# State space layer: four real products kept apart and added by TensorE, late squares and the last group's powers on GpSimd

## What is computed

```python
C_term = C * B[None]
V = jnp.exp(log_dA[:, :, None] * jnp.arange(L))
K = 2.0 * jnp.einsum('chn,hnl->chl', C_term, V).real
```

## Time and profile before

| What | Value |
|---|---|
| Time, median of 3 runs | 1275.31 us (1273.34 to 1276.65) |
| The profiled execution's own time | 1279.39 us |
| Its span | 1277.7 us |
| TensorE, share of the span | 84% |
| VectorE | 56% |
| ScalarE | 37% |
| GpSimd | 19% |
| Granted TensorE clock, mean | 0.906 of full speed |

### The profile page before, as it was taken

One profiled execution on the slowest core, in us unless ns is written; L12 is line 12 of the kernel. 1 busy time (PEld: TensorE's weight loads), 2 busy tenths in 40 slices (PEclk: granted clock), 3 DMA queues, 4 the chain that ended last, 5 costly groups with the idle time before them and its releaser, 6 DMA issues. The chain is left out here.

```text
span 1277.7 us, 22878 instructions
## 1 busy us (share of the span) xinstructions
PE 1074.6 (84%) x8418; PEld 770.7 (60%) x8418; DVE 710.4 (56%) x1761; ACT 472.6 (37%) x938; POOL 248.5 (19%) x337
## 2 busy tenths in 40 slices
PE   1227997987899888989988988988989999999990
PEld 1124665544666456766455744773548999999980
DVE  7992444675555666747577655355443444444445
ACT  2111332444365443355533655433003333333332
POOL 3970000010000001201012100002132333333320
PEclk9857998988999899799987998888889999999995
DMA  5123241019521469022806220114921111111105
GB/s 172 18 52 110 84 168 49 18 33 166 68 75 66 195 215 107 31 79 67 165 1 88 88 67 1 33 34 161 375 91 34 43 35 38 39 34 43 35 30 201
DMA packets 73419, 108.88 MB, mean 85 GB/s; under 512 B 16592, under 2 KB 58336, under 8 KB 72864
## 3 DMA queue, kind: packets, MB, share of 16 engines
q1 hardware_dynamic: 66192, 74.75, 23.4%
q0 software_dynamic: 5280, 14.57, 3.5%
q10 hardware_dynamic: 1840, 18.10, 3.5%
HBM read 83.47 MB, written 40.97 MB: 97 GB/s over the span
## 5 line engine op out<-in xcount | busy, mean ns | idle before, releaser
L1721 DVE TENSOR_REDUCE mx<-scores_ps 128x4 f32<-128x1024 f32 (+1 forms) x160 | 186.9, 1168 | 84.3 <-PE scores_ps L1193 44.0
L1549 ACT ACTIVATE pt<-turned_ps 128x1024 f32<-128x1024 f32 (+1 forms) x160 | 157.6, 985 | 146.8 <-PE turned_ps L1189 97.2
L2266 PEld LDWEIGHTS x_ps<-x_xtT,x_w1s 128*128 128x128 f32 x1248 | 145.3, 192 | 3.4 <-ACT x_xtT L2294 1.5
L2266 PE MATMUL x_ps<-x_xtT,x_w1s 128*128 128x128 f32 x1248 | 145.8, 275 | 1.0 <-ACT x_xtT L2294 1.0
L2280 PE MATMUL x_ps<-x_experts,x_hT 128*128 x624 | 141.0, 379 | 0.0
L2280 PEld LDWEIGHTS x_ps<-x_experts,x_hT 128*128 128x128 f32 x624 | 115.6, 190 | 14.2
L2309 ACT ACTIVATE x_hT<-x_ps,x_b1c 128x128 f32<-128x128 f32 x312 | 84.8, 382 | 16.6 <-issue 13.5
L1179 PE MATMUL turned_ps<-q,k 32*128 32x256 f32 x512 | 69.8, 348 | 22.4 <-DVE mx L1721 12.4
L1179 PEld LDWEIGHTS turned_ps<-q,k 32*128 32x128 f32 x512 | 42.3, 198 | 76.1 <-issue 40.6
L1064 POOL COPY vpad<-v 128x32 f32<-128x32 f32 x128 | 22.8, 223 | 311.2 <-PE ps L1230 296.4
L2329 DVE COPY x_w1s<-x_experts 128x2048 f32 x39 | 55.6, 1429 | 49.1 <-PE x_ps L2266 37.5
(11 more groups left out here) (423 smaller groups left out, 1951.4 us busy)
## 6 DMA issues: line engine op xcount, KB each, us to landing
x_slots<-x_slots ACTq DMA_DIRECT2D x4, 4160.0 KB
wexp<-in_L_ffn_w SPq DMA_DIRECT2D x16, 1024.0 KB, 5.4
x_experts<-in_L_ffn_W SPq DMA_DIRECT2D x16, 1024.0 KB, 13.7
q<-heads SPq DMA_DIRECT2D x48, 128.0 KB, 5.0
k<-heads SPq DMA_DIRECT2D x48, 128.0 KB, 10.0
ha<-h SPq DMA_DIRECT2D x16, 256.0 KB, 3.2
x_pair<-y_rows SPq DMA_DIRECT2D x4, 1024.0 KB, 9.3
heads<-nat_k_hi SPq DMA_DIRECT2D x12, 256.0 KB, 3.9
```

The lines of the kernel that those rows point to most:

```text
L1549: sc.activation(pt[v.index // 2 % (PT_RING // 2)][:, :, 0:wide], turned_ps[:, :, 0:wide], ACT.Exp)\
L1721: v.tensor_reduce(mx[:, u.group % 2, 0:blocks, u.n:u.n + 2].rearrange("p b n -> p n b"), scores_ps[:, :, 0:blocks * (P if u.causal else T) ...
L2266: last = mm(ps[2 * (i % 2) + f // KH][:, f % KH * P:(f % KH + 1) * P], w1s[:, i % 2, c, f * P:(f + 1) * P], xtT[:, i % 2, c, :], start=c = ...
```

## The change

- GpSimd no longer makes the complex product. For each token it writes four real products into `cs` (now four parts): x_r b_r, x_i (-b_i), x_r (-b_i), x_i (-b_r). The subtraction and the addition are gone, as are `csn` and the negation of each group. ScalarE negates `bs` once into `nbs`, in one operation of 128 x 1024.
- TensorE makes four matmuls per token and half in place of two (parts 0 and 1 with the real powers, 2 and 3 with the imaginary ones), all into the same PSUM columns.
- VectorE makes the first four squares only (`EARLY = 4`). GpSimd makes `dk[5]`, `dk[6]` and `dk[7]`, in five operations each.
- VectorE makes the powers of four groups. GpSimd makes those of the last one (`last_powers`), into a buffer of its own, `pw_last`, between the strided products of group 3 and of group 4. `pw_last` lies where the input tile `xin` was. ScalarE still copies the first eight powers of the last group in, at the same place of its order as before, without a wait of its own.

```diff
-    cs = [sb(f"s4_cs{i}", [P, 2, GT, CH, NA]) for i in range(2)]
-    csn = [sb(f"s4_csn{i}", [P, GT, CH, NA]) for i in range(2)]
+    cs = [sb(f"s4_cs{i}", [P, 4, GT, CH, NA]) for i in range(2)]
+    nbs = sb("s4_nbs", [P, 2, HP, NA])
...
+    EARLY = 4
+    sq = sb("s4_sq2", [P, HP])
+
+    def powers_in(g):
+        return pw_last if g == NG - 1 else pw[g % 2]
...
-            pool.wait_ge(squares, 8)
+            pool.wait_ge(squares, EARLY + 1)
+            for k in range(EARLY, 7):
+                cur, nxt = dk[k], dk[k + 1]
+                s.mark(g_.tensor_tensor(nxt[:, 0, :], cur[:, 0, :], cur[:, 0, :], ALU.mult))
+                s.mark(g_.tensor_tensor(sq[:, :], cur[:, 1, :], cur[:, 1, :], ALU.mult))
+                s.step(g_.tensor_tensor(nxt[:, 1, :], cur[:, 0, :], cur[:, 1, :], ALU.mult))
+                s.mark(g_.tensor_tensor(nxt[:, 0, :], nxt[:, 0, :], sq[:, :], ALU.subtract))
+                s.step(g_.tensor_tensor(nxt[:, 1, :], nxt[:, 1, :], nxt[:, 1, :], ALU.add))
+                pool.sem_inc(more_squares, 1)
...
+            pool.sem_inc(bases, 1)
             pool.wait_ge(columns, 4)
-            for g in range(NG):
+            pool.wait_ge(negated, 1)
+
+            def strided(g):
                 tok, count = tokens_of(g), GROUPS[g][1]
                 shape = [P, count, CH, NA]
                 if g >= 2:
                     pool.wait_ge(banks_full, g - 1)
-                    pool.wait_ge(negated, g - 1)
-                cmul(g_, s, [[t[:, i, 0:count] for i in range(2)] for t in (pt1, pt2)],
...
+                for part, (a, b) in enumerate(((xr, br), (xi, nbi), (xr, nbi), (xi, nbr))):
+                    s.mark(g_.tensor_tensor(cs[g % 2][:, part, 0:count], a, b, ALU.mult))
+                s.sync()
                 pool.sem_inc(strides, 1)
+
+            def last_powers():
+                tok, count = tokens_of(NG - 1), GROUPS[-1][1]
+                for k in range(3, 6):
+                    n = 1 << k
+                    base = [p8[:, i, tok, :] if k == 3 else pw_last[:, i, :, 0:n] for i in range(2)]
+                    if k == 3:
+                        pool.wait_ge(eighths, 1)
+                    if k == 4:
+                        pool.wait_ge(heads_in, NG)
+                    d = [dk[k][:, i, tok].unsqueeze(2).to_broadcast([P, count, n]) for i in range(2)]
...
+                    cmul(g_, s, temps, [pw_last[:, i, :, n:2 * n] for i in range(2)], base, d)
+                pool.sem_inc(powers_last, 1)
+
+            for g in range(NG - 1):
+                strided(g)
+            last_powers()
+            strided(NG - 1)
...
-            for k in range(7):
+            for k in range(EARLY):
...
-            for g in range(NG):
+            for g in range(NG - 1):
                 pg, tok, count = pw[g % 2][:, :, 0:GROUPS[g][1]], tokens_of(g), GROUPS[g][1]
...
             def first_powers(g):
-                if g >= 2:
+                if 2 <= g < NG - 1:
                     act.wait_ge(banks_full, g - 1)
...
             for g in range(NG):
-                if g + 1 < NG:
-                    negate(g + 1)
                 act.wait_ge(banks_full, g + 1)
                 if g + 2 < NG:
                     first_powers(g + 2)
...
-                pe.wait_ge(powers, g + 1)
-                pe.wait_ge(negated, g + 1)
+                if g < NG - 1:
+                    pe.wait_ge(powers, g + 1)
+                else:
+                    pe.wait_ge(powers_last, 1)
+                pe.wait_ge(heads_in, g + 1)
+                pe.wait_ge(strides, g + 1)
...
-                    for part in range(2):
+                    for part in range(4):
...
-                                lhs = csn[g % 2][rows, t] if part else cs[g % 2][rows, 0, t]
+                                lhs = cs[g % 2][rows, part, t]
```

More of the change, by code:

```diff
@@ L194, in sb @@
         return ctx.enter_context(nc.sbuf_tensor(name, shape, dt))
-    xin = sb("s4_x", [P, CH, HF, N_STATE, 2])
+    with ExitStack() as before:
+        xin = before.enter_context(nc.sbuf_tensor("s4_x", [P, CH, HF, N_STATE, 2], fp32))
+    pw_last = sb("s4_pw_last", [P, 2, GROUPS[-1][1], NB])
     bin_ = sb("s4_b", [P, HF, N_STATE, 2])
@@ L214, in s4_tokens @@
     p8 = sb("s4_p8", [P, 2, HP, N8])
-    pt1, pt2 = sb("s4_pt1", [P, 2, GT, CH, NA]), sb("s4_pt2", [P, 2, GT, CH, NA])
+    LAST = GROUPS[-1][1]
+    pt1, pt2 = (sb(f"s4_pt{i}", [P, 2, LAST * NB // 2]) for i in (1, 2))
     out = [sb(f"s4_out{i}", [P, TI, NB]) for i in range(4)]
@@ L230, in s4_tokens @@
     squares, powers, strides, negated = (sem(f"s4_{n}") for n in ("squares", "powers", "strides", "negated"))
+    more_squares, powers_last, bases = sem("s4_more_squares"), sem("s4_powers_last"), sem("s4_bases")
     banks_full, copied = sem("s4_banks_full"), sem("s4_copied")
@@ L404, in _ @@
             for k in range(6):
-                act.wait_ge(squares, k + 1)
+                if k <= EARLY:
+                    act.wait_ge(squares, k + 1)
+                else:
+                    act.wait_ge(more_squares, k - EARLY)
                 nc.scalar.copy(factor(k), dk[k][:, :, :]).then_inc(factors, 1)
             def first_powers(g):
-                if g >= 2:
+                if 2 <= g < NG - 1:
                     act.wait_ge(banks_full, g - 1)
[L411 to L417, removed]
+                nc.scalar.copy(powers_in(g)[:, :, 0:GROUPS[g][1], 0:N8], p8[:, :, tokens_of(g), :]).then_inc(heads_in, 1)
             act.wait_ge(eighths, 1)
@@ L421, in _ @@
                 first_powers(g)
-            negate(0)
+            act.wait_ge(bases, 1)
+            nc.scalar.mul(nbs[:, :, :, :], bs[:, :, :, :], -1.0).then_inc(negated, 1)
             for g in range(NG):
-                if g + 1 < NG:
-                    negate(g + 1)
                 act.wait_ge(banks_full, g + 1)
@@ L480, in _ @@
                                 rows = slice(64 * f, 64 * f + 64)
-                                lhs = csn[g % 2][rows, t] if part else cs[g % 2][rows, 0, t]
+                                lhs = cs[g % 2][rows, part, t]
                                 last = nc.tensor.matmul(
                                     ps_out[f][j * M:(j + 1) * M, i * NB:(i + 1) * NB],
-                                    lhs.rearrange("p c a -> p (c a)"), pw[g % 2][rows, part, t, :],
-                                    start=part == 0, stop=part == 1)
+                                    lhs.rearrange("p c a -> p (c a)"), powers_in(g)[rows, part // 2, t, :],
+                                    start=part == 0, stop=part == 3)
                 last.then_inc(banks_full, 1)
```

6 lines of the change are left out of this document (3 added, 3 removed).

## The result

| | before | after |
|---|---|---|
| Median of the runs | 1275.98 us (4 runs) | 1289.41 us (4 runs, 1288.37 to 1290.85) |
| Ratio to before, 95% interval | | 1.0102 (1.008 to 1.0123) |
| The profiled execution's span | 1277.7 us | 1288.4 us |
| First load of the main loop issued at | 96.72 us | 111.48 us |
| From there to the end of the span | 1181.0 us | 1176.9 us |

The change makes the kernel 13.4 us slower (12.6 were forecast). The block ends 14.8 us later in the profile. Of these, 0.8 are not the change's: VectorE's first operation, which waits for the input loads, starts at 5.43 us in the profile after and at 4.64 in the one before. That leaves 14.0. The rest of the program is the same in both, and yet it took 4.1 us less in the profile after.

The account below looks back on a forecast made before the run. The prediction took VectorE to bound the block before, and TensorE's page fetches plus GpSimd's last chain after. The main loop's first load moves from 96.7 to 109.3: 1275.3 + 12.6 = 1287.9 us, range 1279.3 to 1292.

Parts of the forecast that it names:

- VectorE's gain: On VectorE, three squares (3.50 us) and the last group's powers (8.4 us) go; alone this would be 12 us gained.
- GpSimd up to group 0: GpSimd's squares take 7.7 us, its group 0 products end at 42.9, and TensorE starts group 0 at 43.0.
- The page: TensorE fetches instructions one page per 128 matmul records, 3.55 us each (3.3 to 3.8); 512-record groups last 12.6 us.
- The chain behind the heads: GpSimd's last-group work waits for ScalarE's copied heads until 84.2, ends at 99.3; then TensorE 5.5 us, tail 4.4 us.
- Hidden fetch: Rival: TensorE's page fetch is hidden or two are in flight; groups last 7.1 us, 4.0 us later, 1279.3 us; chance 0.13.
- Slower fetch with the stores: Rival: SyncE's overlapping stores slow TensorE's page fetch to 4.5 us, groups last some 15.5 us, about 1297 us; chance 0.10.
- The clock: Rival: more matmuls ahead of the main loop lift its granted clock to full, 4.1 us back, 1283.8 us; chance 0.05.
- A faster last chain: Rival: GpSimd's doublings for the last group cost VectorE's time, 8.4 instead of 14, taking 5 us off, 1283; chance 0.02.
- The number: The block's end moves from 96.7 to 109.3, 12.6 us later; the median of the runs becomes 1287.9 us.

Follow-up runs that it names:

- the shift: The changed kernel with 20 further transposes of the identity on TensorE ahead of group 0: 1290.8 us, 1.0109 of the kernel before.
- undoing the doubling: The changed kernel with parts 0 and 2 of the matmuls alone, GpSimd still writing all four: 1277.3 us, 1.0015 of the kernel before.
- undoing the wait alone: The changed kernel with ScalarE's copy of the last group's first eight powers moved to just behind the eighths: 1284.0 us, 1.0045 of the kernel before.

## Why the prediction was right, step by step

- **VectorE's gain** (3.5 and 8.4 us): as measured, and it bought nothing, as said.
- **GpSimd up to group 0.** Squares took 26.37 - 19.66 = 6.7 us for 7.7 taken: 0.40 to 0.46 us each on 128 contiguous columns. That made up for the late inputs: group 0 started at 43.08 for 43.0. GpSimd was done with it at 42.5 and VectorE at 42.66, so TensorE waited for VectorE and not, as forecast, for GpSimd: here the start came out right partly by luck.
- **The page.** The term on which the sum hangs, 3.55 us each, came out at 3.47 to 4.01. Group 0 took 12.6 us for 12.6, group 2 14.3. I had put 3.8 as the upper end, and moved only the two added pages of a group with it; the first one can be longer too (5.16 us to the first restart for 4.55). TensorE's group 2 ended at 86.38 where 83.8 was forecast: 1.7 us from group 2 itself (first restart 5.16 after its start, then two steps of 4.01), 0.5 from group 1, the rest hand-overs. That is the term that was mis-sized, by some 15% in the longest group; the 2.2 us between 109.3 and 111.48 are these 2.6 less 0.4 in the chain behind them.
- **The chain behind the heads**: wait found where it was said, 15.0 us for 15.0, last group 5.2 for 5.5, tail 4.2 for 4.4.
- **The rivals.** Hidden fetch: excluded by three gaps per group, by the doubled matmuls and by the shift. Slower fetch with the stores: a little slower it was, the stores aren't shown to do it. The clock: it didn't give the loss back, and the windows show the steps as long at both levels. Its price was wrong as well. I had counted 4.1 us back for the loop's start at the full clock; the loop's first 16 large matmuls took 10.02 us in the kernel before, 9.29 in the changed one and 9.35 in the one with the records shifted, whose clock stood at 1.00 for all of them. So at most 0.7 us come from there (the windows below). A faster last chain: no.
- **The number.** The block's end moved by 14.0 us net for 12.6 forecast, the runs by 13.4. That the runs came nearer than the block isn't to the forecast's credit: the rest of the program scatters by more than that.
- **What I had not seen** is that VectorE's last group, before the change, also depended on TensorE's group 2. It didn't enter the sum, since GpSimd took that group over, but it made two of the expectations wrong (5.7 us in the kernel with doubled matmuls).
- **How the loss divides.** Of the 14.0 us net, undoing the doubling gives 13.1 back, and undoing the wait alone 5.6. These aren't parts of a sum: the wait is long because TensorE's groups 0 to 2 are.

Windows over the loop's first 16 large matmuls, in the kernel before, the changed one and the one with the records shifted (columns as above):

```profile
104.04:114.06 10.02, 10.02 (x17) 4.36 (x18) 0.69 (x1) 1.17 (x2) 0.00 (x0) 0.71 0.17 53
119.16:128.45 9.29, 9.29 (x17) 4.08 (x18) 0.69 (x1) 1.17 (x2) 0.00 (x0) 0.76 0.17 57
118.53:127.88 9.35, 9.35 (x17) 4.14 (x18) 0.69 (x1) 1.17 (x2) 0.00 (x0) 1.00 0.17 57
```

## What to carry to other kernels

A small matmul can have a price besides its own time: the instructions it takes, which arrived here in pages, one after the other (3.46 us or more for 2.04 us of matmuls). Before work is moved to an engine that looks idle, look for an "issue" gap in its own stretches; one gap hidden in another engine's period becomes several when the count is doubled, and each then costs in full. Split the work by group: extra matmuls where the period has room for them, none in the last group, where everything is exposed, and let the engines end together.

## What the runs showed of the hardware

- TensorE works off 128 of this layer's matmul records, each with its weight load, per instruction packet, and in a row it gets one packet per 3.46 to 4.01 us (once 4.29); the records themselves take 2.04 or, where the granted clock was just falling, 1.47. In the changed kernel's group 0 the next packet moves about 1 us behind each restart. Whether it could have been asked for before TensorE goes on, these traces can't tell: the page before has only just arrived then.
- The Trainium skill (Runtime: NRT & Kernel Launch, Instruction fetch mechanics) has the cost of a block boundary mostly hidden. The kernel before with its matmuls doubled disagrees: three stalls of 1.31 to 1.96 us in its first group, and the first load 13.0 us later (with VectorE's wait for group 2 in it).
- The granted clock made no difference to the length of such a step: in the kernel with the records shifted, at 1.00 throughout, steps took 3.46 to 4.00 us, and in the one with the heads copied early, at 0.50 or little more, 3.46 to 4.01. 128 records took 2.04 us at 1.00 and at 0.50.
